# TensorE's order in the seven-product tiles of a decoder layer, and where GpSimd builds the block sums

## The chip, the cores and the metric

The kernel runs on one core of one Trainium2 chip. The metric is device time in microseconds (us) of one execution. TensorE does matmuls and transposes, VectorE and ScalarE move and combine what it leaves in its eight accumulation banks, GpSimd works on on-chip memory alone and issues some DMAs, and SyncE issues the other DMAs.

## The reference

One decoder layer for 8 sequences of 128 tokens, width 512, with a layer norm behind each of its three parts:

```python
x = _layernorm(x + _L0_attn_ref(x, L0_attn_Wq, L0_attn_Wk, L0_attn_Wv, L0_attn_Wo), axis=-1)
x = _layernorm(x + _L0_xattn_ref(x, ctx_4096, mask_BxSxS2_bk0, ...), axis=-1)
x = _layernorm(x + _L0_ffn_ref(x, L0_ffn_W_base, L0_ffn_b_base, ...), axis=-1)
```

The middle one is most of the time: cross attention with 32 heads of width 128.

```python
h_q = (x @ w_q.T).reshape(b, lq, H, DH)
h_k = (key_value_states @ w_k.T).reshape(b, lk, H, DH)
h_v = (key_value_states @ w_v.T).reshape(b, lk, H, DH)
score = jnp.einsum('bqhd,bkhd->bhqk', h_q, h_k)
score = score + position_bias[None]
score = jax.nn.softmax(jnp.where(m, score, -jnp.inf), axis=-1)
attn = jnp.einsum('bhqk,bkhd->bqhd', jnp.where(m, score, 0.0), h_v).reshape(b, lq, H * DH)
out = attn @ w_out.T
```

## The kernel before

Every projection is made of three matmul passes over split operands: a value is a high part and a low part (`hi`, `lo`), and the products hi·hi, lo·hi and hi·lo are summed in a bank. ScalarE writes the high part of a weight block, VectorE the low part.

The cross attention goes over 16 groups of two heads (`g` 0 to 15). A group has four tiles (`s` 0 to 3), one for a head and a half of the sequences. Tile number `n` is 4g+s. In tile n TensorE takes the scores of n, the transposes of the probabilities of n−1, the product of those with v (`pv`), two new v projections (`project_v`), and two output products (`output`) of earlier heads; between them lie the projections of q and k for later tiles.

In groups 0 and 1 ("plain") a tile projects q and k with twelve matmuls each (`project_q`, `project_k`). From group 2 on a group's q and k come from a scheme with seven block products in place of eight: `product_1` to `product_7`, each once for q (`w` = 0) and once for k (`w` = 1), with six matmuls of 128x512. Five of the right factors for each group are not the inputs but sums of input blocks, named S1k, S2k, S3k, S4k, S2q, S3q, S4q (and S1q, which stays on chip). GpSimd makes these sums once while groups 0 and 1 run, SyncE writes them to DRAM (`keep`, semaphores `s_kept`), and in every group GpSimd issues seven loads of 1 MB each into two ring slots (`load_sums`). A slot is reloaded when the product that read it is done: slot 0 holds S2q, S1k, S4k, S3k in turn, slot 1 holds S2k, S4q, S3q. The ring slots lie over four quarters of the buffer `stage`, `area(0)` to `area(3)`, in which GpSimd also builds the sums; `mem.u` is a further block of that size, used later by ScalarE for the copies of product 1 (`copy_p1`).

What sets the order is code written out by hand for each engine; each engine takes its instructions in that order and waits on semaphores. Two chains matter here. First, `bias_mask(g, s)` on GpSimd adds mask and bias for tile n into `bm`; VectorE's `masked_scores` of tile n waits for it (`s_bm`). GpSimd makes these adds between the block sums. Second, ScalarE in a plain tile takes `exps(n)` (which waits for VectorE's maxima), `copy_q`, `copy_k`, then `copy_prT(n-1)`; TensorE's `pv(n-1)` in the same tile waits for that last copy. VectorE turns the products into q and k (`sum_c11` and its like), and `normalise(n)` writes the probabilities.

A wait that both parts of the text speak of, in `product_6`:

```python
pe.wait_ge(s_op, done(OPS, g, "T2"))
pe.wait_ge(s_ring[SLOT_OF[name]], loaded(g, name))
pe.wait_ge(s_sum[w], done(SUMS, g, "C11"))
```

The weights' own sums T1 to T4 are GpSimd's (`three_turns`, `last_turn`), and T1 waits until the block A11 was split by VectorE.

Of the kernel before, what the change touches and what calls it, by code (L numbers as in the profile page):

```python
# [14 lines left out]
ALU = mybir.AluOpType  # L15
# [748 lines left out]
def layer(nc, a, sem, banks, mem, prev_a, out_d):  # L764
# [6 lines left out]
    with ExitStack() as ctx:  # L771
# [56 lines left out]
        BLOCKS = ("S1k", "S2k", "S4k", "S3k", "S3q", "S2q", "S4q")  # L828
# [13 lines left out]
        def loaded(g, name):  # L842

            order = SLOT_ORDER[SLOT_OF[name]]
            return 16 * len(order) * g + 16 * (order.index(name) + 1 - len(order) * SEVEN)
# [83 lines left out]
        def _(sp):  # L929
# [54 lines left out]

            sp.wait_ge(s_wv, 1)
# [10 lines left out]
            keep("S1k", stage[:, 0:2 * HALF * T], stage[:, 2 * HALF * T:4 * HALF * T])  # L996
            keep("S2k", stage[:, 0:2 * HALF * T], stage[:, 6 * HALF * T:8 * HALF * T])
# [4 lines left out]
            u_all = mem.u[:].rearrange("p i n -> p (i n)")  # L1002
            keep("S4k", stage[:, 2 * HALF * T:4 * HALF * T], u_all)
            keep("S3k", stage[:, 0:2 * HALF * T], stage[:, 4 * HALF * T:6 * HALF * T])
            keep("S3q", stage[:, 0:2 * HALF * T], stage[:, 6 * HALF * T:8 * HALF * T])
            sp.wait_ge(s_bm, TILES * 2)
            load_bias(2)
            keep("S2q", stage[:, 0:2 * HALF * T], u_all)
            keep("S4q", stage[:, 6 * HALF * T:8 * HALF * T], stage[:, 2 * HALF * T:4 * HALF * T])
# [28 lines left out]
        def _(pool):  # L1038
# [20 lines left out]
            def block_lo(name, out, raw, hi):  # L1059
                for c in range(2):  # L1060
                    nc.gpsimd.tensor_tensor(out[:, c], raw[:, c], f32(hi[:, c]), ALU.subtract).then_inc(s_ready, 1)  # L1061
                    pool.wait_ge(s_ready, 2 * BLOCKS.index(name) + c + 1)

# [17 lines left out]
            def k_first():  # L1081
                pool.wait_ge(prev_a.s_wout, B)
                pool.wait_ge(prev_a.s_xnlo, B)
                combine(U_, area(3), f32(quarter(cT[0], 0, 0)), ALU.add)
                combine(U_, U_, f32(quarter(cT[1], 0, 0)), ALU.add)
                hi_of(area(0, F32R), U_)
                block_lo("S1k", area(1, F32R), U_, area(0, F32R))

            def k_fourth():
# [1315 lines left out]
```

## Time and profile before

| | |
|---|---|
| median of 3 runs | 1098.26 us (1098.13 to 1098.43) |
| the profiled execution | 1096.46 us, of which the span from first to last instruction is 1094.5 us |
| mean granted TensorE clock | 0.988 |
| busy TensorE, VectorE | 1033.9 us (94%), 747.5 us (68%) |
| busy ScalarE, GpSimd | 500.6 us (46%), 488.0 us (45%) |

Busy time says who is nearest to being the bound. What a change is worth is read from the idle stretches of that engine and from what ended them. In this span the first self attention ends near 205 us, groups 0 and 1 run until about 318 us, groups 2 to 15 until about 1030 us, and the feed-forward part is the rest.

### The profile page before, as it was taken

The numbers are of one execution on the slowest core, as the hardware profiler recorded it, in microseconds if no ns is written. First come the engines' busy times: TensorE is split into PE (matmuls) and PEld (weight loads), VectorE is DVE, ScalarE is ACT, GpSimd is POOL, SyncE is SP. The second block draws the span as 40 slices with busy tenths as digits, with TensorE's granted clock in tenths as the row PEclk, the third lists the DMA queues.
The fourth block names the chain that finished last, engine by engine and source line by source line (L and its number), as shares of the span: only waits on it lengthen the run. The fifth ranks groups of instructions, "written<-read, shape, count | busy, mean of one in ns | idle before, by whom it ended". The sixth has DMA issues, their size and how long they took to land.

```text
span 1094.5 us, 20557 instructions
## 1 busy us (share of the span) xinstructions
PE 1033.9 (94%) x6354; PEld 895.0 (82%) x6354; DVE 747.5 (68%) x2269; ACT 500.6 (46%) x1377; POOL 488.0 (45%) x576
## 2 busy tenths in 40 slices
PE   7899988999689999999999999999999999999995
PEld 6677767888578888888888888888888888888884
DVE  6799988664557575757576666767575757576883
ACT  4889886454324343534343434444343435342421
POOL 7676665799954232423333242423242324232142
PEclk9999999999889999999999999999999999999998
DMA  4301002233375546372727374646455463737001
GB/s 150 126 21 50 2 1 69 78 117 120 124 259 185 193 157 235 115 249 101 258 98 286 99 255 142 242 142 227 164 186 192 157 236 113 249 101 243 19 20 58
DMA packets 44588, 159.77 MB, mean 146 GB/s; under 512 B 4736, under 2 KB 21504, under 8 KB 31616
## 3 DMA queue, kind: packets, MB, share of 16 engines
q0 software_dynamic: 14528, 105.91, 27.3%
q1 hardware_dynamic: 30016, 53.32, 14.5%
q8 instruction: 22, 0.36, 0.1%
q14 instruction: 22, 0.18, 0.0%
HBM read 149.78 MB, written 9.44 MB: 145 GB/s over the span
## 4 chain that ended last, share of the span: by engine, by line
PE 61%; POOL 13%; DVE 9%; DMA 8%; issue 7%; ACT 1%; POOLq 0%; DVEq 0%; SPq 0%; ACTq 0%
PE bank L1940 22%; PE bank L760 13%; PE bank L2094 11%; DMA ring<-block_sums 7%; PE bank L2081 4%; PE bank L2064 4%; PE bank L2112 3%; POOL stage L1053 3%; DVE sm L481 2%; PE bank L2071 2%; POOL u L1053 2%; POOL stage L1061 1%; POOL bm L1045 1%; POOL stage L1057 1%; POOL pool_gate L1070 1%
## 5 line engine op out<-in xcount | busy, mean ns | idle before, releaser
L1045 POOL TENSOR_TENSOR bm<-mask,bias 128x512 f32<-128x512 f32 x64 | 84.0, 1314 | 219.6 <-DVE nmx L1589 217.4
L1334 ACT ACTIVATE pr<-sm,nmx 128x128 f32<-128x128 f32 x256 | 99.8, 391 | 172.2 <-DVE nmx L1589 172.2
L1638 DVE TENSOR_TENSOR acc<-acc,bank 128x512 f32<-128x512 f32 x128 | 86.2, 684 | 78.0 <-PE bank L2094 78.0
L1070 POOL TENSOR_TENSOR pool_gate<-eps 128x1 f32<-128x1 f32 x96 | 44.1, 459 | 186.3 <-PE bank L1940 186.3
L1940 PE MATMUL bank<-ring,wqk_hi 128*128 128x512 f32 x392 | 112.1, 408 | 12.7 <-DMA ring<-block_sums 7.6
L1327 ACT COPY v<-bank 128x256 f32<-128x256 f32 x124 | 45.9, 370 | 127.7 <-PE bank L760 80.8
L2094 PE MATMUL bank<-wo_hi,at_hi 128*128 128x512 f32 x256 | 100.5, 393 | 0.3 <-DVE acc L1638 0.3
L2094 PE MATMUL bank<-wo_hi,at_lo 128*128 128x512 f32 x256 | 100.1, 391 | 0.1
L2094 PE MATMUL bank<-wo_lo,at_hi 128*128 128x512 f32 x256 | 100.0, 391 | 0.0
L1607 DVE TENSOR_TENSOR wqk_lo<-qk_raw,wqk_hi 128x512 fp32r<-128x512 f32 x98 | 88.4, 903 | 10.5 <-ACT wqk_hi L1364 10.5
L760 PE MATMUL bank<-wv_hi,cT_hi 128*128 128x256 f32 x512 | 88.9, 296 | 0.2 <-DVE wv_lo L1895 0.2
L1940 PEld LDWEIGHTS bank<-ring,wqk_hi 128*128 128x128 f32 x392 | 67.3, 191 | 25.2 <-issue 9.1
L760 PE MATMUL bank<-wv_hi,cT_lo 128*128 128x256 f32 x512 | 82.5, 284 | 0.0
L760 PE MATMUL bank<-wv_lo,cT_hi 128*128 128x256 f32 x512 | 82.3, 283 | 0.0
L1601 DVE TENSOR_TENSOR at_lo<-bank,at_hi 128x512 fp32r<-128x512 f32 x64 | 43.9, 686 | 55.3 <-ACT at_hi L1348 55.3
L1342 ACT COPY prT<-bank 128x512 f32<-128x512 f32 x64 | 37.3, 583 | 92.2 <-PE bank L2071 92.2
L760 PEld LDWEIGHTS bank<-wv_hi,cT_hi 128*128 128x128 f32 x512 | 72.7, 190 | 4.6 <-issue 0.4
L760 PEld LDWEIGHTS bank<-wv_hi,cT_lo 128*128 128x128 f32 x512 | 70.8, 192 | 0.0
L2064 PEld LDWEIGHTS bank<-kT,qT 128*128 128x128 f32 x512 | 66.7, 191 | 4.8
L760 PEld LDWEIGHTS bank<-wv_lo,cT_hi 128*128 128x128 f32 x512 | 70.5, 191 | 0.0
L2081 PE MATMUL bank<-prT,v 128*128 128x128 f32 x512 | 67.8, 275 | 1.3 <-ACT prT L1342 1.3
L2064 PE MATMUL bank<-kT,qT 128*128 128x128 f32 x512 | 67.3, 274 | 0.0
(289 smaller groups left out, 2620.8 us busy)
## 6 DMA issues: line engine op xcount, KB each, us to landing
ring<-block_sums POOLq DMA_DIRECT2D x98, 1024.0 KB, 5.2
qk_raw<-in_wqk SPq DMA_DIRECT2D x56, 256.0 KB, 5.6
o_raw<-in_wo SPq DMA_DIRECT2D x16, 512.0 KB, 3.3
v_raw<-in_wv SPq DMA_DIRECT2D x15, 512.0 KB, 8.7
block_sums<-stage SPq DMA_DIRECT2D x12, 512.0 KB, 3.2
acc<-in_x POOLq DMA_DIRECT2D x1, 2048.0 KB, 8.2
qk_raw<-in_wqk SPq DMA_DIRECT2D x4, 512.0 KB, 5.8
bias<-in_bias SPq DMA_DIRECT2D x16, 128.0 KB, 2.0
```

The source lines that it names most:

```text
L760: ins = nc.tensor.matmul(out, lhs, rhs, start=start and i == 0, stop=i == len(pairs) - 1)
L1045: nc.gpsimd.tensor_tensor(bm[:, s % 2], mask[:, HALF * (s // HG):HALF * (s // HG + 1), :], bias[:, i:i + 1, :].broadcast_to([P, HALF, T]), ...
L1053: made.link(nc.gpsimd.tensor_tensor(out[:, c], in0[:, c], in1[:, c], op))
L1070: nc.gpsimd.tensor_tensor(pool_gate[:, BLOCKS.index(name):BLOCKS.index(name) + 1], eps[:, 0:1], eps[:, 0:1], ALU.add)
L1327: nc.scalar.copy(v[:, b, :], PX[b % 2][:, 0:HG * DH2]).then_inc(s_vc, 1)
L1334: e = nc.scalar.activation(pr[:, s % 2, k], sm[:, s % 2, k], ACT.Exp, bias=nmx[:, s % 2, k:k + 1], accum_out=sums[:, s % 2, k:k + 1])
L1607: nc.vector.tensor_tensor(part_of(slot, 1), block_of(qk_raw, raw), f32(part_of(slot, 0)), ALU.subtract).then_inc(s_op, 1)
L1638: nc.vector.tensor_tensor(acc[:, b], acc[:, b], PX[b % 2][:], ALU.add).then_inc(s_acc, 1)
L1940: ins = nc.tensor.matmul((PQ, PK)[w][:], lhs, rhs, start=i == 0, stop=i == len(pairs) - 1)
L2064: ins = nc.tensor.matmul(S[s % 2][:, tok], qT[:, s % 2, tok], kT[:, s % 2, tok], start=True, stop=True)
L2081: ins = nc.tensor.matmul(PO[:, k * T:(k + 1) * T], v[:, half * HALF + k, i * DH2:(i + 1) * DH2], prT[:, k], start=True, stop=True)
L2094: ins = nc.tensor.matmul(PX[b % 2][:], at[p][:, half, i, tok], wo[q][:, i, :], start=k == 0 and (p, q) == PARTS[0], stop=k == HG - 1 and ( ...
```

## The change

It has two parts.

The order in the tiles of the seven-product scheme is now: scores, transposes of tile n−1, v, two products, `pv`, v, two products, outputs. Before, two products stood ahead of the transposes and the other two around the second v. In the last tile of a group product 6 for q comes ahead of `pv`, with the two products 2; in the first tile the two outputs alternate with the products 3. ScalarE copies the transposed probabilities ahead of the exponentials in these tiles, and VectorE's sums are put in an order to fit.

The block sums of the context are now made from the unsplit context. SyncE reads its first half again (two DMAs of 512 KB into `area(0)` and `area(1)`), ahead of the weights of group 1. GpSimd's order is new: `k_sums` has 8 instructions and `q_third` 6, and `bias_mask(1, 0)` stands behind the four splits of k and `q_third`. The last sum, S2q, is left in ring slot 0, from where product 6 of group 2 reads it.

```diff
+            sp.wait_ge(prev_a.s_wout, B)
+            for i in range(2):
+                sp.dma_start(area(i), mem.context_half(a["cT"], 0)[:, 2 * i:2 * i + 2]).then_inc(s_c_in, 16)
             sp.wait_ge(s_wv, 1)
             load_v(1)
...
-            def k_differences():
+            def k_sums():
                 pool.wait_ge(s_clo[0], 2)
                 pool.wait_ge(s_clo[1], 2)
-                combine(area(2), area(2), f32(quarter(cT[0], 0, 0)), ALU.subtract)
-                combine(area(2), area(2), f32(quarter(cT[1], 0, 0)), ALU.subtract)
-                combine(area(3), area(3), area(2), ALU.add)
+                pool.wait_ge(s_c_in, 48)
+                combine(area(0), area(2), area(0), ALU.subtract)
+                combine(area(2), area(2), area(3), ALU.add)
+                combine(area(3), area(3), area(0), ALU.add)
+                combine(area(1), area(1), area(3), ALU.subtract)
...
-            k_differences()
+            k_sums()
             bias_mask(0, 3, True)
-            k_first()
-            k_fourth()
-            k_second()
-            bias_mask(1, 0, False)
+            k_first_split()
+            k_second_split()
             k_fourth_split()
             k_third_split()
+            q_third()
+            bias_mask(1, 0, False)
+            q_second()
             bias_mask(1, 1, False)
-            q_third()
-            q_second()
-            bias_mask(1, 2, False)
             q_third_split()
             q_fourth()
-            bias_mask(1, 3, False)
             q_first()
-            q_second_split()
+            bias_mask(1, 2, False)
             q_fourth_split()
             q_first_split()
-            for name in BLOCKS[-2:]:
-                wait_kept(pool, name)
+            three_turns(SEVEN)
+            q_second_split()
             pool.wait_ge(s_s1q, 1)
-            load_sums(SEVEN, "S2q")
             load_sums(SEVEN, "S2k")
-            three_turns(SEVEN)
+            bias_mask(1, 3, False)
...
                 if isinstance(g, int) and g == SEVEN and w == 0:
-                    wait_kept(act, "S2q")
+                    wait_kept(act, "S3k")
...
+                scores(n, s, False, None if plain else g)
+                transposes(n - 1, sp)
+                new_v(g, n, b, c, weights)
+                if s == 0:
+                    product_5(g, 1)
+                    product_5(g, 0)
+                if s == 1:
+                    product_7(g, 0)
+                if s == 2:
+                    pair(product_4, g)
+                if s == 3:
+                    pair(product_2, g + 1)
+                    if not plain:
+                        product_6(g + 1, 0)
+                pv(n - 1, sp, head, v_ready, False)
+                new_v(g, n, b + 1, c + 1, weights)
+                if s == 0:
+                    product_3(g, 0)
+                    out(0)
+                    product_3(g, 1)
+                    out(1)
+                    return
```

TensorE at the start of a group from 3 on (tile s = 0). L2064 is the scores, L1940 with `ring_49` product 5 for k, which reads S1k, L2071 the transposes, L760 the v projection. Before:

```order
L2064 MATMUL bank<-kT,qT 128x128 [waits b_negmax]
L2064 MATMUL bank<-kT,qT 128x128 x3
L1964 REGISTER_ALU
L1968 ISA [waits b_operand]
L1969 REGISTER_ALU [waits b_sums_in_even]
L1940 MATMUL bank<-ring_49,wqk_hi 128x512 [waits b_k_product_summed]
L1940 MATMUL bank<-ring_49,wqk_hi 128x512 x3
L1940 MATMUL bank<-ring_49,wqk_lo 128x512 x2
```

The same place now, where L2068 is the scores, L2075 the transposes and L1941 the product:

```order
L2068 MATMUL bank<-kT,qT 128x128 [waits b_negmax]
L2068 MATMUL bank<-kT,qT 128x128 x3
L2075 MATMUL bank<-ident,pr 128x128 [waits b_probs]
L2075 MATMUL bank<-ident,pr 128x128 x3
L2185 REGISTER_ALU
L2186 ISA [waits b_wv]
L2187 REGISTER_ALU [waits b_acc]
L760 MATMUL bank<-wv_hi,cT_hi 128x256 [waits b_v_copied]
L760 MATMUL bank<-wv_hi,cT_hi 128x256 x3
L760 MATMUL bank<-wv_lo,cT_hi 128x256 x4
L760 MATMUL bank<-wv_hi,cT_lo 128x256 x4
```

The wait for the load of S1k (`b_sums_in_even`) moved behind the transposes and one v projection.

TensorE in the last tile of a group (s = 3), product 6 for q and `pv`. Before, with L2081 for `pv`:

```order
L2081 MATMUL bank<-prT,v 128x128 [waits b_at_lo,b_v_copied]
L2081 MATMUL bank<-prT,v 128x128 x3
L1958 REGISTER_ALU
L1959 ISA [waits b_operand]
L1940 MATMUL bank<-ring_49,wqk_hi 128x512 [waits b_q_product_summed,b_sums_in_even]
```

Now, with L2085 for `pv` and the products 2 for k just ahead:

```order
L1941 MATMUL bank<-cT_hi,wqk_lo 128x512 x2
L1959 REGISTER_ALU
L1963 ISA [waits b_operand]
L1941 MATMUL bank<-ring_49,wqk_hi 128x512 [waits b_q_product_summed,b_sums_in_even]
L1941 MATMUL bank<-ring_49,wqk_hi 128x512 x3
L1941 MATMUL bank<-ring_49,wqk_lo 128x512 x2
L2080 REGISTER_ALU [waits b_prT]
L2085 MATMUL bank<-prT,v 128x128 [waits b_at_lo,b_v_copied]
```

Product 6 for q moved ahead of `pv`, right behind products 2, whose sum it waits for (`b_q_product_summed`).

GpSimd while groups 0 and 1 run, from the wait for the context on. L1057 is `combine`, L1061 and L1065 the two steps of a split, L1049 `bias_mask`. Now:

```order
L1057 TENSOR_TENSOR stage<-stage 128x512 [waits b_ctx_in,b_ctx_lo_odd,b_ctx_lo_even]
L1057 TENSOR_TENSOR stage<-stage 128x512 [waits b_sums_made] x7
L1049 TENSOR_TENSOR bm<-mask,bias 128x512 [waits b_negmax,b_sums_made]
...
L1061 CAST u<-stage 128x512 [waits b_sums_kept_even,b_sums_ready]
...
L1057 TENSOR_TENSOR stage<-xnT_hi 128x512 [waits b_sums_ready]
L1057 TENSOR_TENSOR stage<-xnT_hi 128x512 [waits b_sums_made]
L1057 TENSOR_TENSOR stage<-stage,xnT_lo 128x512 [waits b_sums_made] x4
L1049 TENSOR_TENSOR bm<-mask,bias 128x512 [waits b_negmax,b_bias_in,b_sums_made]
```

The first instruction now waits for the DMA of the context (`b_ctx_in`), and the second `bm` shown, that of tile 4, stands behind 16 instructions of splits and 6 of `q_third`.

## Rows read from the trace of the kernel before

**Rows 1.** Waits from 284 to 318 us: us in total, times, longest

```profile
ACT u L1370 <- DMA block_sums<-u: 13.3, 1, 13.3
...
PE bank L1940 <- ACT u L1370: 8.1, 1, 8.1
...
PE bank L1940 <- DVE wqk_lo L1607: 4.5, 1, 4.5
```

**Rows 2.** Windows on TensorE: length, busy (instructions), granted clock, DMA share, GB/s

```profile
297.40:301.80 4.40, 4.31 (x12) 0.62 0.92 331
...
309.20:315.90 6.70, 6.63 (x25) 0.61 0.51 152
```

**Rows 3.** Timeline of TensorE, scores of four tiles and the next: start, us

```profile
629.26 1.05 PE L2064 MATMUL bank<-kT,qT 128*128 128x128 f32 x8
...
643.53 1.05 PE L2064 MATMUL bank<-kT,qT 128*128 128x128 f32 x8
...
667.51 1.05 PE L2064 MATMUL bank<-kT,qT 128*128 128x128 f32 x8
...
680.92 1.05 PE L2064 MATMUL bank<-kT,qT 128*128 128x128 f32 x8
```

**Rows 4.** Line 1071: first the issue at 624.4 us (S1k), then S4k

```profile
DMA to landing us min/median/max: 6.4/6.4/6.4
...
L1071 POOL DMA_DIRECT2D ring<-block_sums x1: 577/577/577, 633.1 to 633.1; - x1
...
DMA to landing us min/median/max: 5.1/5.1/5.1
```

**Rows 5.** Timeline of a tile s = 1, and VectorE's first instruction behind `normalise`

```profile
591.87 1.05 PE L2064 MATMUL bank<-kT,qT 128*128 128x128 f32 x8
...
594.62 1.08 PE L1940 MATMUL bank<-ring,wqk_hi 128*128 128x512 f32 x4
...
596.01 1.05 PE L2081 MATMUL bank<-prT,v 128*128 128x128 f32 x8
...
596.85 0.69 DVE L1607 TENSOR_TENSOR wqk_lo<-qk_raw,wqk_hi 128x512 fp32r<-128x512 f32 x1
...
598.34 1.08 PE L1940 MATMUL bank<-ring,wqk_hi 128*128 128x512 f32 x4
```

**Rows 6.** SyncE's second DMA from 210 us on; a load of 1 MB behind one of 512 KB

```profile
210.65 0.37 SPq L935 DMA_DIRECT2D v_raw<-in_wv  x1
...
stage<-in_cT SPq DMA_DIRECT2D x1, 1024.0 KB, 7.5
```

**Rows 7.** Timeline of GpSimd: sums, a mask, one split

```profile
209.81 2.64 POOL L1053 TENSOR_TENSOR stage<-stage,cT_hi 128x512 f32<-128x512 f32 x2
...
218.31 1.30 POOL L1045 TENSOR_TENSOR bm<-mask,bias 128x512 f32<-128x512 f32 x1
...
244.31 1.29 POOL L1057 CAST stage<-u 128x512 fp32r<-128x512 f32 x2
...
248.40 1.29 POOL L1057 CAST stage<-stage 128x512 fp32r<-128x512 f32 x2
```

**Rows 8.** DMAs issued at 232.5 to 233 us, writes of S1k

```profile
block_sums<-stage SPq DMA_DIRECT2D x2, 512.0 KB, 3.1
```

**Rows 9.** Timeline of tile 4 on VectorE, ScalarE and TensorE

```profile
246.04 0.28 DVE L1584 CUSTOM_DVE_ANT_0 sm<-bank,bm 128x128 f32<-128x128 f32 x1 [0.21 <-issue]
...
247.21 0.41 ACT L1334 ACTIVATE pr<-sm,nmx 128x128 f32<-128x128 f32 x1 [4.44 <-DVE nmx L1589]
...
248.84 0.59 ACT L1317 COPY qT<-bank 128x512 f32<-128x512 f32 x1
...
253.26 1.06 PE L2081 MATMUL bank<-prT,v 128*128 128x128 f32 x8
```

**Rows 10.** Timeline of tile 6: the scores, and VectorE's splits of A11 and A22

```profile
271.71 1.05 PE L2064 MATMUL bank<-kT,qT 128*128 128x128 f32 x8
...
279.98 3.18 DVE L1607 TENSOR_TENSOR wqk_lo<-qk_raw,wqk_hi 128x512 fp32r<-128x512 f32 x2 [0.20 <-ACT wqk_hi L1364]
```

More of the change, by code:

```diff
@@ L827, in layer @@
         SLOT_ORDER = [[n for n in SLOT_OF if SLOT_OF[n] == k] for k in range(2)]
-        BLOCKS = ("S1k", "S2k", "S4k", "S3k", "S3q", "S2q", "S4q")
+        BLOCKS = ("S1k", "S2k", "S4k", "S3k", "S3q", "S4q", "S2q")
         UNITS = ("p1", "p2", "p6", "p5", "p3", "p7", "p4")
@@ L995, in _ @@
             load_v(2)
-            keep("S1k", stage[:, 0:2 * HALF * T], stage[:, 2 * HALF * T:4 * HALF * T])
-            keep("S2k", stage[:, 0:2 * HALF * T], stage[:, 6 * HALF * T:8 * HALF * T])
+            u_all = mem.u[:].rearrange("p i n -> p (i n)")
+            flat = [stage[:, k * 2 * HALF * T:(k + 1) * 2 * HALF * T] for k in range(4)]
+            keep("S1k", u_all, flat[2])
+            keep("S2k", u_all, flat[3])
+            keep("S4k", flat[2], flat[1])
+            keep("S3k", u_all, flat[0])
             for i in range(HG):
@@ L1001, in _ @@
                 load_block(SEVEN, name)
[L1002 to L1005, printed above, removed]
+            keep("S3q", flat[0], flat[3])
+            keep("S4q", flat[0], flat[1])
+            keep("S2q", *[f32(mem.ring[0][:, p].rearrange("p c n -> p (c n)")) for p in range(2)])
             sp.wait_ge(s_bm, TILES * 2)
             load_bias(2)
-            keep("S2q", stage[:, 0:2 * HALF * T], u_all)
-            keep("S4q", stage[:, 6 * HALF * T:8 * HALF * T], stage[:, 2 * HALF * T:4 * HALF * T])
             sp.wait_ge(s_wo, 2)
@@ L1269, in first_half @@
                 bias_mask(g, 3, False)
+            wait_kept(pool, "S2q")
             second_half(SEVEN)
@@ new lines, in seven_step, with short_step @@
+                if s == 2 and not last:
+                    pair(product_1, g + 1)
+                if s == 3 and plain:
+                    product_6(g + 1, 0)
+                if s == 3:
+                    product_6(g + 1, 1)
+                out(0)
+                out(1)
+            def short_step(g, s):
+                n, sp = TILES * g + s, (s - 1) % TILES
+                scores(n, s, False, g)
+                if s == 1:
+                    pair(product_7, g)
+                transposes(n - 1, sp)
+                for j in range(2):
+                    pe.wait_ge(s_acc, 2 * n - 5 + j)
+                    output((HALF + 2 * s + j) % B, s // HG ^ 1 if s < 2 else 0, (1, 0) if s < 2 else (0, 1))
+                    if j == 0:
+                        pv(n - 1, sp, FRESH_B[sp], B * g + HALF * (sp // HG + 1), False)
@@ L2202, in step @@
                         continue
+                    if last and s in (1, 3):
+                        short_step(g, s)
+                        continue
+                    if not plain or (s == 3 and not plain_next):
+                        seven_step(g, s, last, plain)
+                        continue
                     sp = (s - 1) % TILES
                     had_out = not (first and s < 3)
-                    head = heads_of(first or (s == 0 and plain))[sp]
-                    order = (0, 1) if s >= 2 or plain else (1, 0)
@@ L2213, in out @@
+                    for j in range(2):
+                        pe.wait_ge(s_vc, 2 * n + HALF + j + 1)
                         if j == 0 and s == 2:
                             pe.wait_ge(s_wo, g + 1)
[L2215 to L2223 removed]
@@ L2238, in step @@
-                    for j in range(2):
-                        pe.wait_ge(s_vc, 2 * n + HALF + j + (-1 if moved else 1))
-                        out(j)
-                    if plain and not plain_next and s == 2:
-                        product_1(g + 1, 0)
-                        product_1(g + 1, 1)
+                        output((HALF + 2 * s + j) % B, 0 if s >= 2 else 1, (0, 1), n if j == 0 and s in (0, 2) else None)
+                    if not plain_next and s == 2:
+                        pair(product_1, g + 1)
```

175 lines of the change are left out of this document (84 added, 91 removed).

## The prediction

> **What bounds the kernel now.** I read the page's busy shares first (TensorE 94%), then TensorE's waits, then the timeline around the longest. TensorE is the bound almost everywhere, so only its idle stretches and slow stretches can be won. They lie in two places.
>
> The first is where group 2 takes over from the plain groups. ScalarE's copy of product 1 waited 13.3 us for the write of S2q to DRAM, and TensorE waited 8.1 us for that copy, then 4.5 us for a VectorE split that hung on GpSimd's late weight sums [rows 1]. Behind each stall the granted clock was low: 4.40 us at 0.62 and 6.70 us at 0.61, a mix of the 1.2 and 2.4 GHz levels [rows 2]. At 0.62 the work done in 4.40 us is worth 2.7 us, so 1.7 us were lost, and in the second window 2.6 us. The place costs 8.1 + 4.5 + 1.7 + 2.6 = 16.9 us.
>
> The second recurs in each group. The tile s = 0 lasts 643.53 − 629.26 = 14.27 us, and the tile s = 3, which has the same instructions in number and shape (scores, transposes, two v, four products, `pv`, two outputs), 680.92 − 667.51 = 13.41 us [rows 3]. The 0.86 us between them is the wait of product 5 for S1k, whose load took 6.4 us [rows 4]. In a group of 51.66 us that is all the idle time.
>
> **The change, steady groups.** The matmuls are the same in number. In the order scores, transposes, v, product, which the tile s = 1 already has, the product starts at +2.75 us from the scores and takes 596.01 − 594.62 = 1.39 us; from `pv` to the product behind the next v it is 2.33 us [rows 5].
>
> - Product 5 for k now starts at +2.75 in place of about +0.8, and product 6 for q, which frees the slot, ends earlier: before at 2 × 1.39 + 1.39 behind transposes, v and `pv`, now without `pv` ahead (0.8 us). The load of S1k gets 1.9 + 0.8 us more against a lateness of 0.86. The wait goes: −0.86 us a group.
> - Product 6 for q now starts at 2.75 + 2 × 1.39 = +5.53 in the last tile, and waits for VectorE's sum of product 2. VectorE now takes `normalise` first and comes free at 596.85 − 591.87 = +4.98; the sum takes as long as the 0.69 us beside it and ends at +5.67 [rows 5]. That is 0.14 late, and the start behind a wait costs some 0.1 to 0.2 us more, as the weight load can't run ahead: +0.3 us. Below nothing it can't go; if ScalarE's exponentials slip it is 0.6.
> - Product 3 for k starts at 5.53 + 2.33 + 1.39 + 1.37 (an output, six matmuls of the same width) = +10.6. Its block S4k is loaded when product 5 for k is done, at +4.14, through GpSimd's queue, so issued near +5.0. It took 5.1 us when issued at 633.13 [rows 4], so it lands at +10.1, and the weight load would be due at +10.4. I take 0.06 us for it; it is the thinnest cover of the change.
> - Outputs, copies by ScalarE ahead of the exponentials (the transposes end before VectorE has the maxima), and the reordered adds lie under TensorE's work: nothing.
>
> Net −0.86 + 0.3 + 0.06 = −0.5 us a group. The tile s = 0 counts 13 times (groups 3 to 15) and so does product 6: −6.5 us, between −2.6 (0.2 a group) and −8 (0.6).
>
> **The change, start of group 2.** GpSimd has three `combine` less (6 instructions), TensorE needs S2q later and from the ring slot where it was made, and ScalarE no longer waits for its write. But the sums start later.
>
> - The context copies are issued behind `load_o(0)`, where the second DMA now stands, at 210.65 [rows 6]. A load of 1 MB of this context behind one of 512 KB took 7.5 us [rows 6], so both halves are there at 218.2. GpSimd was ready at 209.8 [rows 7]. It waits 8.4 us, more than the 8.4 us that the six instructions saved are worth (209.81 to 218.31 for six, 1.4 each [rows 7]).
> - From there: `k_sums`, 8 × 1.4 = 11.2, to 229.4. Mask of tile 3, 1.3, to 230.7. Split of S1k 4.1 (244.31 to 248.40 for one [rows 7]), to 234.8. The next split writes into `mem.u`, which S1k's write reads: 0.4 for the second issue and 3.1 for the landing [rows 8], to 238.3. Three splits, 12.3 and 0.3 for a wait on S2k's write, to 250.9. `q_third`, 6 × 1.4 = 8.4, to 259.3. Mask of tile 4, 1.3, to 260.6.
> - VectorE wanted that mask at 246.04 [rows 9]; it is 14.6 us late. Behind it in a plain tile: maxima 1.17 (to 247.21), exponentials 1.63 (to 248.84), `copy_q`, `copy_k` at a pitch of about 0.5, `copy_prT` 0.6 as the copies beside it, together 4.4. So `pv` starts at 265.0 in place of 253.26 [rows 9]: +11.7 us. Low clock behind the stall: 1.7 and 2.6 stand in the rows for the old ones; I take 2.5, at most 3.4. Shift 14.2.
> - GpSimd's next pieces have room: masks of tiles 5 and 6 come before their shifted tiles. Tile 6 starts at 285.9. VectorE's split of A11 ended 9.9 us behind its scores (279.98 + 1.6 − 271.71 [rows 10]): 295.8. Three weight sums at 1.4, S2q's split 4.1: 304.1. Mask of tile 7 to 305.9, when its scores (302.5) are 3.4 old. Maxima 1.2, exponentials 1.6, the copy of T2 0.6, `normalise` and the split of T2 about 1.6: 310.9. Product 6 would be due at 302.5 + 5.53 + 2.33 = 310.4: a wait of 0.5, in place of the old 4.5. S2k, issued near 304.6, lands near 310 to 312, in time.
> - Tile 8 starts near 316.6 (302.5 + 13.4 + 0.5, and 0.2 for a start behind a wait). S1k is issued near 312.9 and by 6.4 us [rows 4] lands at 319.3, just when product 5 is due. GpSimd's queue and SyncE's weight loads are fuller at this place, so I allow 0.8 us of wait, between 0 and 1.7.
>
> So the old 16.9 us and the 0.86 go, and 11.7 + 2.5 + 0.5 + 0.8 come. That is 17.8 − 15.5 = 2.3 us gained. Bounds: GpSimd and VectorE slow each other (VectorE's split takes 1.6 us in the one place and 0.69 in the other [rows 10, 5]); with GpSimd's mean piece at 1.6 the mask comes at 264, +3.4 and some clock, a loss near 2; with every piece at 1.3 it comes at 259, a gain near 4.
>
> **A rule beside it.** The load of 1 MB behind 512 KB took 7.5 us [rows 6]. The Trainium skill (DMA: Bandwidth & Descriptors, "Specifications" and "Anatomy of one DMA") puts the fixed part at about 2 us and the ceiling of one core's DMA at 435 GB/s; by an estimate from it the context is there near 216, 2.2 us sooner, and the time would be 1087.3 us. No row here shows that rate for this load.
>
> **The sum.** −2.3 − 6.5 = −8.8 us. The profiled execution (1096.46 us, its span 1094.5) becomes 1087.7, and its distance of 1.8 us to the median of the three runs is kept: 1098.26 − 8.8 = 1089.5 us.
>
> **The rivals.**
>
> 1. *The mask is not late enough to matter.* If the context were there when GpSimd is ready, the chain would end 8.4 us sooner and leave a stall of 3.3 us with no lasting loss of clock: −8.4 − 2.5 = −11 beyond the forecast, 1078.6 us. For it: SyncE's queue was empty when the copies are issued. Against it: the copies can't be issued before the last transposes of the first part, at 210.2. Chance 0.14.
> 2. *Slower: S4k decides.* The thinnest cover is product 3 for k. The load is issued near +5.0 and must land by +10.4, so the point is 5.4 us; it took 5.1, but S1k's took 6.4 with other loads in flight [rows 4]. At 6.4 each of the 14 first tiles waits 1.0 and some 0.15 for the start: +16 us, 1105 us. It turns the sign from 6.1 us on. For it: S3q's and S4k's loads stand nearer together now. Against it: S4k's neighbour has nearly landed at that point. Chance 0.14.
> 3. *Nothing measurable.* The chain on GpSimd ends at 264 to 266 and the groups give only 0.2: 2 + 1 − 2.6, about 1098.5 us. For it: GpSimd's pieces doubled beside VectorE's. Against: VectorE idles while it waits for this very mask. Chance 0.12.
>
> The forecast has 0.60.
>
> **How the numbers follow.** The forecast's own range is 1084 to 1094.5 (−4 and −8 from the low bounds with some of the clock; +2 and −2.6 with some clock on the other side). The range 1077.5 to 1099 takes in rivals 1 and 3 and leaves out rival 2 and some tails, under 2 in 10. A change within 0.2% (2.2 us) is about what can't be told from none. Faster: 0.60 + 0.14 + a little of rival 3 and less 0.02 of tails, 0.74. Same: 0.10. Slower: 0.16.
>
> **What the changed profile would show.** GpSimd's first `combine` waits until about 218 for a DMA. The mask of tile 4 ends near 260.6. TensorE waits once near 253 to 265 for `prT`, and the stalls of 8.1 and 4.5 us are gone. In each group the tile s = 0 lasts 13.4 to 13.6 us, and product 6 in the last tile waits 0.1 to 0.4 us for VectorE. It is wrong if the context lands much off 218, if a plain tile has more slack than 4.4 us behind its mask, or if a ring load is waited for in every group.

## The result and the profile after

The changed kernel takes 1117.73 us (1116.52 to 1119.63), against 1098.20 us of the kernel before on the same chip: ratio 1.0182, interval 1.0164 to 1.0200, slower. The forecast was 1089.5 us, and the range ended at 1099. The profiled span grew from 1094.5 to 1115.6 us, 21.1 us. TensorE runs the same 6354 matmuls, and its busy time grew by 6.6 us (1033.9 before):

```profile
span 1115.6 us, 20550 instructions
...
PE 1040.5 (93%) x6354; PEld 895.5 (80%) x6354; DVE 730.6 (65%) x2269; ACT 498.0 (45%) x1377; POOL 487.9 (44%) x569
```

So the work didn't grow. Two thirds of the loss is idle time, and the rest is matmuls that ran slower (the mean granted clock went from 0.988 to 0.985, and it is low behind long stalls, as shown below). The starts of the scores of each tile, read from TensorE's timeline of both kernels, say where (these are differences of rows like those of [rows 3]):

| stretch | before, us | after, us | difference |
|---|---|---|---|
| tile 0 to tile 9 | 136.58 | 143.14 | +6.6 |
| tiles s = 0 of groups 3 to 15, mean of 13 | 14.26 | 14.51 | +0.25 |
| tiles s = 1, mean of 13 | 10.60 | 10.67 | +0.07 |
| tiles s = 2, mean of 13 | 13.38 | 13.70 | +0.32 |
| tiles s = 3, mean of 13 | 13.41 | 13.73 | +0.32 |

(The tiles s = 1 to 3 are those of groups 2 to 14, so the four rows are one stretch without a gap.) The groups lose 0.96 us each, 12.5 us in 13. The rest is 0.9 us ahead of tile 0, where nothing was changed, and 1.2 us in the last group. Tile 0 starts anywhere from 195.7 to 197.6 us in the twelve traces of this document, so the 0.9 us is scatter. The 1.2 us stand in the last group of every run with the new order, and most of them are two products in its tile s = 1 that wait 1.5 us together, where one waited 0.6 before. The forecast had −6.5 for the groups and −2.3 for the start of group 2.

**The start of group 2.** Waits from 205 to 330 us in the kernel after (us in total, times, longest), to be held against [rows 1]:

```profile
DVE spare L51 <- POOL bm L1049: 17.1, 1, 17.1
...
PE bank L2085 <- ACT prT L1339: 15.6, 3, 13.9
...
POOL stage L1057 <- DMA stage<-in_cT: 8.7, 1, 8.7
...
POOL bm L1049 <- issue: 7.3, 1, 7.3
...
POOL u L1061 <- DMA block_sums<-stage: 4.1, 1, 4.1
...
PE bank L1941 <- DMA ring<-block_sums: 3.8, 1, 3.8
```

The old stalls of 8.1 and 4.5 us are gone. In their place stand `pv` behind the mask of tile 4 (13.9) and product 5 behind the load of S1k (3.8). GpSimd's timeline shows the chain behind the first (start, us, what it waited for):

```profile
209.04 1.74 POOL L1049 TENSOR_TENSOR bm<-mask,bias 128x512 f32<-128x512 f32 x1
219.43 13.87 POOL L1057 TENSOR_TENSOR stage<-stage 128x512 f32<-128x512 f32 x8 [8.65 <-DMA stage<-in_cT]
...
243.69 1.29 POOL L1061 CAST u<-stage 128x512 fp32r<-128x512 f32 x2 [4.08 <-DMA block_sums<-stage]
...
264.00 1.26 POOL L1049 TENSOR_TENSOR bm<-mask,bias 128x512 f32<-128x512 f32 x1
...
308.74 0.61 POOL L1075 DMA_DIRECT2D ring<-block_sums  x1 [0.30 <-POOL ring L1065]
309.38 1.30 POOL L1049 TENSOR_TENSOR bm<-mask,bias 128x512 f32<-128x512 f32 x1
317.93 1.30 POOL L1049 TENSOR_TENSOR bm<-mask,bias 128x512 f32<-128x512 f32 x1 [7.26 <-issue]
```

Read from the top: GpSimd is ready at 210.8 and waits for the context until 219.4; `k_sums` takes 13.87 us; the write of S1k is waited for; the mask of tile 4 ends at 265.3. TensorE's timeline of that tile:

```profile
247.34 1.05 PE L2068 MATMUL bank<-kT,qT 128*128 128x128 f32 x8
...
269.73 2.08 PE L2085 MATMUL bank<-prT,v 128*128 128x128 f32 x8 [13.91 <-ACT prT L1339]
...
276.68 0.49 PE L2068 MATMUL bank<-kT,qT 128*128 128x128 f32 x3
```

The tile lasts 29.34 us, 15.95 more than before. The `pv` takes 2.08 us in place of 1.05: the granted clock is low behind the stall (0.61 from 269 to 275 us).

**A steady group.** The tile s = 0 that starts at 537.21, the longest, lasts 15.41 us. On TensorE, product 5 for k, product 3 for q and the first output run without a gap, and then:

```profile
537.21 1.05 PE L2068 MATMUL bank<-kT,qT 128*128 128x128 f32 x8
...
539.96 1.08 PE L1941 MATMUL bank<-ring,wqk_hi 128*128 128x512 f32 x4
...
545.08 1.08 PE L1941 MATMUL bank<-ring,wqk_hi 128*128 128x512 f32 x4
...
549.73 1.20 PE L1941 MATMUL bank<-ring,wqk_hi 128*128 128x512 f32 x4 [1.73 <-DMA ring<-block_sums]
```

The product at +2.75 us (539.96) waits for nothing, as the prediction said: the wait for S1k is gone. The one that waits is product 3 for k, for S4k. That load was issued at 541.73 (the line of the load, from issue to landing):

```profile
L1075 POOL DMA_DIRECT2D ring<-block_sums x1: 580/580/580, 541.7 to 541.7; - x1
...
DMA to landing us min/median/max: 8.0/8.0/8.0
```

This is group 6 (tile 24). The load took 8.0 us where [rows 4] has 5.1. In groups 3 to 14 of this trace it took 6.0 to 8.0 us, the middle one 7.2. SyncE's timeline shows what is new beside it: the weight block d goes out at 540.41, 1.3 us ahead of S4k, because VectorE now splits T3 before its other work. Before, it went out 0.2 to 1.0 us behind the load of S4k.

```profile
540.41 4.38 SPq L964 DMA_DIRECT2D qk_raw<-in_wqk  x2
```

The 0.32 us of s = 3 are the wait of product 6 for q, and those of s = 2 a wait that I hadn't looked for. VectorE and TensorE around the start of a tile s = 2 (scores at 563.22):

```profile
564.11 0.60 PE L2075 MATMUL bank<-ident,pr 128*128 128x128 f32 x4
564.85 0.73 PE L760 MATMUL bank<-wv_hi,cT_hi 128*128 128x256 f32 x4
```

```profile
562.11 0.67 DVE L1610 TENSOR_TENSOR u<-bank,u 128x512 f32<-128x512 f32 x1
562.71 1.42 DVE L1573 TENSOR_TENSOR wv_lo<-v_raw,wv_hi 128x1024 fp32r<-128x1024 f32 x1
564.05 1.27 DVE L1636 TENSOR_TENSOR acc<-acc,bank 128x512 f32<-128x512 f32 x2
```

The v projection could start at 564.47 (0.36 behind the transposes, as in the other tiles) and starts at 564.85. Its bank is free only when the first of the two adds is done, near 564.7. In the old order two products 4 stood ahead of it and covered this.

### The profile page after: what moved, and what is told of

Its sections match the earlier page's. It is cut to its first block, busy times and chain, and to the rows that moved or that the text cites. A ratio compares the mean times of both kernels' runs of the same rounds, so it can differ in the third digit from the quotient of the medians.

```text
span 1115.6 us, 20550 instructions
## 1 busy us (share of the span) xinstructions
PE 1040.5 (93%) x6354; PEld 895.5 (80%) x6354; DVE 730.6 (65%) x2269; ACT 498.0 (45%) x1377; POOL 487.9 (44%) x569
## 4 chain that ended last, share of the span: by engine, by line
PE 39%; issue 12%; DMA 8%; DVE 7%; POOL 3%; ACT 2%; DVEq 0%; POOLq 0%; ACTq 0%
PE bank L1941 17%; DMA ring<-block_sums 8%; PE bank L760 7%; PE bank L2098 7%; PE bank L2116 3%; PE bank L2085 2%; POOL bm L1049 2%; PE bank L2068 2%; ACT pr L1331 2%; DVE wqk_lo L1605 1%; DVE acc L1636 1%; PE bank L2075 1%; DVE u L1610 1%; DVE wv_lo L1573 1%; DVE sm L1582 1%
## 5 line engine op out<-in xcount | busy, mean ns | idle before, releaser
L1049 POOL TENSOR_TENSOR bm<-mask,bias 128x512 f32<-128x512 f32 x64 | 99.5, 1555 | 205.9 <-DVE nmx L1587 196.5
L1074 POOL TENSOR_TENSOR pool_gate<-eps 128x1 f32<-128x1 f32 x96 | 38.4, 400 | 214.4 <-PE bank L1941 214.3
L1941 PE MATMUL bank<-ring,wqk_hi 128*128 128x512 f32 x392 | 110.4, 403 | 20.4 <-DMA ring<-block_sums 15.5
L1605 DVE TENSOR_TENSOR wqk_lo<-qk_raw,wqk_hi 128x512 fp32r<-128x512 f32 x98 | 79.0, 807 | 33.4 <-ACT wqk_hi L1361 33.4
L1941 PEld LDWEIGHTS bank<-ring,wqk_hi 128*128 128x128 f32 x392 | 67.5, 190 | 41.0 <-DMA ring<-block_sums 16.8
L760 PE MATMUL bank<-wv_hi,cT_hi 128*128 128x256 f32 x512 | 92.5, 303 | 1.8 <-DVE acc L1636 0.3
L2085 PEld LDWEIGHTS bank<-prT,v 128*128 128x128 f32 x512 | 67.3, 193 | 22.0 <-ACT prT L1339 17.1
L2085 PE MATMUL bank<-prT,v 128*128 128x128 f32 x512 | 68.7, 278 | 16.2 <-ACT prT L1339 16.2
L760 PE MATMUL bank<-wv_lo,cT_hi 128*128 128x256 f32 x512 | 82.2, 283 | 0.0
L760 PE MATMUL bank<-wv_hi,cT_lo 128*128 128x256 f32 x512 | 82.2, 283 | 0.0
L760 PEld LDWEIGHTS bank<-wv_hi,cT_hi 128*128 128x128 f32 x512 | 69.7, 191 | 5.0 <-issue 4.7
L2068 PEld LDWEIGHTS bank<-kT,qT 128*128 128x128 f32 x512 | 66.7, 191 | 4.8
L760 PEld LDWEIGHTS bank<-wv_hi,cT_lo 128*128 128x128 f32 x512 | 70.6, 191 | 0.0
L760 PEld LDWEIGHTS bank<-wv_lo,cT_hi 128*128 128x128 f32 x512 | 70.2, 190 | 0.0
L1345 ACT CAST at_hi<-bank 128x512 fp32r<-128x512 f32 x64 | 37.7, 589 | 69.5 <-PE bank L2085 69.5
```

The costliest lines, as they stand in the source:

```text
L760: ins = nc.tensor.matmul(out, lhs, rhs, start=start and i == 0, stop=i == len(pairs) - 1)
L1049: nc.gpsimd.tensor_tensor(bm[:, s % 2], mask[:, HALF * (s // HG):HALF * (s // HG + 1), :], bias[:, i:i + 1, :].broadcast_to([P, HALF, T]), ...
L1074: nc.gpsimd.tensor_tensor(pool_gate[:, BLOCKS.index(name):BLOCKS.index(name) + 1], eps[:, 0:1], eps[:, 0:1], ALU.add)
L1345: nc.scalar.copy(at[0][:, s // HG, i], PO[:]).then_inc(s_ah, 1)
L1605: nc.vector.tensor_tensor(part_of(slot, 1), block_of(qk_raw, raw), f32(part_of(slot, 0)), ALU.subtract).then_inc(s_op, 1)
L1941: ins = nc.tensor.matmul((PQ, PK)[w][:], lhs, rhs, start=i == 0, stop=i == len(pairs) - 1)
```

## Experiments

Runs of one batch share a chip and their runs of the kernel before; medians of before went from 1096.2 to 1098.2 us between batches, so I compare ratios to before. The changed kernel has 1.0182.

**1 and 2: the two halves apart.** The first has the new tile order of TensorE (here its core), ScalarE and VectorE on the old sums. The second has the new `BLOCKS`, `keep` and GpSimd order (here its core) and the read of S2q from the ring, on the old tile order.

```diff
+                    if not plain or (s == 3 and not plain_next):
+                        seven_step(g, s, last, plain)
+                        continue
```

```diff
-            k_differences()
+            k_sums()
...
-            load_sums(SEVEN, "S2q")
...
-                pe.wait_ge(s_ring[SLOT_OF[name]], loaded(g, name))
+                if isinstance(g, int) and g == SEVEN and w == 0:
+                    pe.wait_ge(s_ready, 2 * len(BLOCKS))
```

> The kernel before with the new tile order alone (TensorE, ScalarE, VectorE); GpSimd and SyncE build the block sums as before. Theory A (the groups lose about 1.0 us each because of the tile order: product 3 for k waits for the load of S4k, the tiles s = 2 and s = 3 wait 0.3 us each for VectorE): 1098.2 + 12.5, and at the start of group 2 the old stalls with some change of either sign, so 1108 to 1113 us, and the tiles s = 0, 2, 3 last about 14.5, 13.7 and 13.7 us as in the changed kernel. Theory B (the groups lose because of where the last sums lie and what the ring loads meet, that is because of both parts together): the tiles of the groups from 3 on last 13.4 to 13.8 us with no ring wait, and the time is 1092 to 1099 us.

> The kernel before with the new building of the block sums alone (SyncE reads the context again, GpSimd's new order, S2q left in the ring); the tile order is the old one. Theory A (this part costs what the first groups lost, the groups from 3 on stay at 14.26, 10.60, 13.38 and 13.41 us a tile): a wait of about 14 us for the mask of tile 4, the old stalls of 8.1 and 4.5 us mostly gone, 1102 to 1107 us. Theory B (the old order in tiles 7 and 8 wants product 6 and S1k sooner than the new one, so the late S2q costs more here): over 1109 us.

The order alone took 1111.69 us, 1.0117 (1.0081 to 1.0152); the sums alone 1103.68 us, 1.0060 (1.0041 to 1.0078). The two add up to 1.0177, so within these intervals no interaction shows. In the order alone the tiles of groups 3 to 15 last 14.75, 10.60, 13.75 and 13.74 us, and tile 0 to 9 takes 0.9 us less than before. In the sums alone they last 14.14, 10.60, 13.38 and 13.41 us, as before, and tile 0 to 9 takes 7.9 us more. In the order alone the load of S4k took 6.9 to 8.2 us in groups 3 to 14, but 5.1 us in group 6. Theory A held on both. The stall of the sums alone, with the old order around it:

```profile
267.31 2.07 PE L2081 MATMUL bank<-prT,v 128*128 128x128 f32 x8 [13.94 <-ACT prT L1339]
```

**3: the masks moved up.** All four masks of group 1 go ahead in GpSimd's order, the first into the wait for S1k's write.

```diff
             k_first_split()
+            bias_mask(1, 0, False)
             k_second_split()
             k_fourth_split()
             k_third_split()
+            bias_mask(1, 1, False)
             q_third()
-            bias_mask(1, 0, False)
             q_second()
-            bias_mask(1, 1, False)
+            bias_mask(1, 2, False)
...
-            bias_mask(1, 2, False)
+            bias_mask(1, 3, False)
             q_fourth_split()
```

> The changed kernel with the four masks of group 1 moved up among GpSimd's block sums, the first one into the 4.1 us in which GpSimd waits for the write of S1k. Theory A (what bounds the first groups is GpSimd's whole chain from the context's landing at 219 to the split of S2q at 308; the mask's wait only hides it): tile 4 lasts 13.4 us, but product 6 of group 2 then waits 6 to 10 us for S2q, and the kernel gains 4 to 9 us of 1117.7: 1109 to 1114 us. Theory B (the late mask of tile 4 is the cost itself, as the prediction priced it, 11.7 + 2.5 and more): gain of 14 to 16 us, 1102 to 1104 us, with no long wait at product 6.

It took 1114.99 us, 1.0155 (1.0127 to 1.0183), 2.7 thousandths better than the changed kernel, though the intervals overlap. Tile 4 is back at 13.38 us, but tile 7 went from 15.65 to 33.22:

```profile
307.84 2.05 PE L1941 MATMUL bank<-ring,wqk_hi 128*128 128x512 f32 x4 [10.59 <-issue]
...
315.73 2.04 PE L1941 MATMUL bank<-ring,wqk_hi 128*128 128x512 f32 x4 [4.99 <-issue]
```

Product 6 for q waits for the split of S2q, which ends near 307.8 on GpSimd, and product 6 for k for the load of S2k, issued at 308.04 and landed 7.6 us later. So the mask was only where the lateness showed first; what bounds this place is GpSimd's whole chain. Theory A's mechanism held. Its gain (4 to 9) was too high, and the time lies 1 us above its range. One reason is the second wait, which I had left out. Another stands in the trace: tile 0 to 9 takes 2.7 us less than in the changed kernel, but tile 12 lasts 17.01 us in place of 14.23. There product 3 for k waits 1.8 us for S4k, and the mean granted clock from 384 to 392 us is 0.84.

**4: block d behind S4k.**

```diff
-                sp.wait_ge(s_op, done(OPS, g, "T3"))
-                load_block(g + 1, "d")
                 sp.wait_ge(s_op, done(OPS, g, "T4"))
+                load_block(g + 1, "d")
                 load_block(g + 1, "b")
```

> The changed kernel, but SyncE loads the weight block d only when T4 is split, 2.7 us behind the issue of S4k in place of 1.3 us ahead of it. Theory A (the load of S4k took 8.0 us in place of 5.1 because this 256 KB stands ahead of it): S4k lands in 5 to 6.5 us, product 3 for k waits 0 to 0.3 us, the tiles s = 0 last 13.4 to 13.8 us, and the time is 1105 to 1110 us against 1117.7. Theory B (it is the sum of the traffic around it, S4q, v and the blocks, wherever block d stands): S4k still takes over 7 us, the tiles s = 0 last about 14.5 us, 1116 to 1119 us.

1112.50 us, 1.0146 (1.0122 to 1.0171). The load of S4k in group 6 (issued at 539.04):

```profile
L1074 POOL DMA_DIRECT2D ring<-block_sums x1: 580/580/580, 539.0 to 539.0; - x1
...
DMA to landing us min/median/max: 5.5/5.5/5.5
```

5.5 in place of 8.0 in this group. Over groups 3 to 14 the load took 5.2 to 7.6 us, the middle one 6.5 (in the changed kernel 7.2), so one group says little. The tiles s = 0 fell from 14.51 to 13.93 us on average; six of 13 are at 13.4, the others still wait. Block d was half of it. Neither theory held: 13.93 us and 1112.5 us lie above the ranges of A and below those of B.

**5: VectorE's two places.**

```diff
                     sum_c22(g, 1)
-                    sum_z(g, 1)
+                    accumulate(n, 0, (HALF + 2 * s) % B)
                     lo(wv, v_raw, s_wv_h, s_wv, g + 2)
+                    sum_z(g, 1)
+                    accumulate(n, 1, (HALF + 2 * s + 1) % B)
+                    return
...
-                    normalise(n, s, link)
                     sum_c11(g + 1, 0)
+                    normalise(n, s, link)
                     sum_c11(g + 1, 1)
```

> The changed kernel with two changes of VectorE's order: in the tile s = 1 the first add of the outputs and the split of wv come ahead of the sum z for k, and in the tile s = 3 the sum C11 for q comes ahead of normalise. Theory A (the v projection of s = 2 waits 0.37 us for its bank behind these, and product 6 for q 0.27 us behind normalise): the tiles s = 2 and s = 3 go from 13.70 and 13.73 to 13.4 us, 13 times each, and the kernel from 1117.7 to 1109 to 1111 us if nothing else moves. Theory B (a wait of the same length appears behind it, for the split of wv in s = 2 or for the sum u1 in s = 0): the tile s = 2 stays above 13.6, or s = 0 grows by as much, 1115 us or more.

1106.66 us, 1.0084 (1.0052 to 1.0116). The tiles s = 2 and s = 3 last 13.33 and 13.37 us, 0.36 each less than in the changed kernel, and s = 0 stays at 14.43. Both waits were as named. The time is 2 us below the expected range; the two tiles explain 9.5 of the 10.8 us gained.

**6: v behind S4k too.** The edit of 4, and v behind the blocks.

```diff
-                sp.wait_ge(s_wv, g + 1)
-                load_v(g + 1)
...
                 load_block(g + 1, "d")
                 load_block(g + 1, "b")
+                sp.wait_ge(s_wv, g + 1)
+                load_v(g + 1)
```

> The changed kernel with SyncE's loads of d, b and then v all behind the split of T4, so that neither d nor the 512 KB of v lie ahead of S4k. Theory A (S4k's landing is set by what was issued ahead of it): S4q lands in 6 to 7 us in place of 8.9, S4k in 5.1 to 5.5 in place of 8.0, all tiles s = 0 last 13.4 us, 13 times 1.1 us less than the changed kernel, 1102 to 1105 us against 1117.7. Theory B (v behind S4k shares its bandwidth as well, and only the sum counts): no better than with block d alone behind S4k, s = 0 at 13.9 us on average, 1110 to 1114 us.

1101.46 us, 1.0038 (1.0024 to 1.0053). All 13 tiles s = 0 last 13.42 or 13.43 us. The landing of all loads of the sums from 340 to 1020 us, the changed kernel's first, then this one's:

```profile
DMA to landing us min/median/max: 5.0/5.2/9.1
```

```profile
DMA to landing us min/median/max: 5.0/5.2/7.6
```

The S4k of group 6, issued at 535.71, took 5.1 us, and in groups 3 to 14 it took 5.1 to 5.4. So the landing of S4k was set by d and v, which were issued ahead of it, and 13.42 us is what the prediction had promised for this tile. Two things stay open. With v away, S4q, which goes out 6.9 us ahead of S4k from GpSimd too, lands in 5.5 to 7.6 us in place of 8.3 to 9.1; whether v holds up S4k itself or by way of S4q isn't shown. And v now goes out 3.9 us behind S4k, so the two overlap for some 1.3 us only: the run shows what it is worth to issue v late, and not whether the order of issue or the traffic in the same time counts.

**7: the order alone, mended.** Experiment 1 with the edits of 5 and 6.

> The new tile order with the old building of the block sums, and the three things that cost it time mended: d, b and v behind the split of T4, and VectorE's two places. Theory A (these three waits are all that the order costs): the tiles last 13.4, 10.6, 13.4 and 13.4 us, that is 50.8 in place of 51.65 us a group before, 13 times 0.85 = 11 us, with the start of group 2 as in the order alone (0.9 us less than before): 1085 to 1088 us against 1097.5 to 1098. Theory B (the mended waits come back somewhere, a load of v or of the blocks that is now late, or a slower clock): 1092 us or more.

1085.72 us (1084.55 to 1086.95), ratio 0.9895 (0.9875 to 0.9915): faster than both kernels. The tiles last 13.43, 10.84, 13.33 and 13.37 us, 50.97 a group in place of 51.65, which is 8.9 us in 13 groups, and tile 0 to 9 takes 2.5 us less. Of TensorE's waits from 340 to 1020 us this is all that is left:

```profile
PE bank L1946 <- issue: 1.5, 2, 1.2
PE bank L2077 <- DVE pr L1595: 0.9, 1, 0.9
PE bank L1946 <- DMA ring<-block_sums: 0.5, 1, 0.5
```

The tile s = 1 is 0.24 us longer than before. It is the price of moving v: it now goes out 1.3 us ahead of S3q, the next load, in place of 6.6 us ahead of S4k. In tile 9, the longest with 12.09 us, product 7 for q waited for S3q, which was issued at 326.61 and took 7.9 us:

```profile
334.54 1.19 PE L1946 MATMUL bank<-ring,wqk_hi 128*128 128x512 f32 x4 [1.24 <-DMA ring<-block_sums]
```

In a steady group S3q is issued 9.65 us behind the start of the tile s = 0 and wanted 16.2 us behind it, so it has 6.5 us. In tile 57, with 11.43 us, it took 7.2; in tiles 21 and 25, with 10.60, it took 6.1 and 6.0. Experiment 6 has the same waits, among others in tiles 9, 17 and 21.

**8: the old order with v late.** Could the load's side alone have won the 0.86 us?

```diff
-                sp.wait_ge(s_wv, g + 1)
-                load_v(g + 1)
                 sp.wait_ge(s_op, done(OPS, g, "T3"))
                 load_block(g + 1, "d")
                 sp.wait_ge(s_op, done(OPS, g, "T4"))
                 load_block(g + 1, "b")
+                sp.wait_ge(s_wv, g + 1)
+                load_v(g + 1)
```

> The kernel before with nothing changed but SyncE's load of v, which stands behind the block b. The old wait for S1k in the tile s = 0 (0.86 us a group) is attacked from the load's side. Theory A (S1k took 6.4 us because blocks a, c and v were issued beside it, and v is the largest): S1k lands in 5.2 to 5.8 us, the tiles s = 0 last 13.4 to 13.7 us in place of 14.26, 13 times 0.6 to 0.85, and the kernel gains 8 to 11 us: 1087 to 1090 us. Theory B (it is the blocks a and c that are issued with it that count, v comes 1.4 us later): S1k still takes 6.2 to 6.4 us and nothing is gained, 1097 to 1099 us.

1095.73 us, 0.9989 (0.9975 to 1.0002): no difference. The tiles s = 0 stay at 14.28 us, and S1k takes 6.1 to 6.5 us in groups 3 to 14, where it took 6.0 to 6.4 before. Theory B: v went out 1.4 us behind S1k there and held it little. The same load matters for S4k since by then it is 6.6 us old and still not down (8.8 us in the changed kernel). So the gain of 7 needs the new order. (The time is 1 us below what theory B expected, with the kernel before at 1096.85 in this batch.)

**9: no reload of the context.** The sums are then made from whatever the two areas hold; only the time is read.

```diff
-            sp.wait_ge(prev_a.s_wout, B)
-            for i in range(2):
-                sp.dma_start(area(i), mem.context_half(a["cT"], 0)[:, 2 * i:2 * i + 2]).then_inc(s_c_in, 16)
...
-                pool.wait_ge(s_c_in, 48)
+                pool.wait_ge(prev_a.s_wout, B)
```

> The changed kernel without SyncE's second load of the context's first half and without the wait for it; the sums are made from what area(0) and area(1) hold, so the output is another and only the time is read. It asks what the lateness of the context costs. Theory A (GpSimd's chain starts 8 to 9 us sooner, at 211, and all of it comes sooner by that): the wait for the mask of tile 4 falls from 13.9 to some 5 us, tile 2 is back at 13.6 us, and the kernel is 9 to 12 us faster than 1117.7: 1106 to 1109 us. Theory B (the chain is held by other things, the write of S1k and VectorE's large splits beside it, and gives the 8 us back on its way): the wait in tile 4 stays over 9 us, the gain is under 6 us.

1108.58 us, 1.0117 (1.0100 to 1.0134). GpSimd starts at once, and TensorE's wait in tile 4 shrinks from 13.91 to 8.09 us:

```profile
209.87 12.05 POOL L1054 TENSOR_TENSOR stage<-stage 128x512 f32<-128x512 f32 x8
```

```profile
260.77 2.08 PE L2082 MATMUL bank<-prT,v 128*128 128x128 f32 x8 [8.09 <-ACT prT L1336]
```

The kernel gains 6.5 thousandths, 7 us, between the two theories (9 to 12, and under 6). `k_sums` starts 9.6 us sooner, and the mask of tile 4 comes 264.00 − 255.05 = 8.95 us sooner. The wait shrinks by 5.8 us only, since TensorE is at this place 3.1 us sooner as well. Tile 2 went from 15.18 to 13.39 us: in the changed kernel the load of v stood behind the context's in SyncE's order, was issued at 212.51 and took 8.0 us, and `pv` waited 1.1 us. The context's lateness is thus worth 7 us. Without it the ratio is that of the order alone (1.0117 both), so even then the new sums win nothing.

**10: everything mended.** The whole change with the edits of 3, 5 and 6.

> The whole change with everything mended that the runs showed: the masks moved up, SyncE's d, b and v behind the split of T4, VectorE's two places. Theory A (the gains add up: 2.7 of the masks, 13 times 1.1 in s = 0, 13 times 0.7 in s = 2 and 3): 1117.7 - 26 = about 1091.5 us, 1089 to 1094, that is faster than before but 4 to 8 us slower than the order alone mended (1085.7), the price of the new block sums. Theory B (with the order mended the late S2q and the loads of the first groups cost more): over 1095 us.

1090.69 us, 0.9949 (0.9935 to 0.9963). Inside theory A's range. The groups last as in 7 but for s = 1 (10.66), and tile 7 takes 32.85 us. The mended order with the old sums is 5.4 thousandths faster, near 6 us. So the new sums cost about what experiment 2 said (6.0 thousandths), though here with the masks moved up.

## Why the prediction was wrong

**The step that failed** is the one that gave product 3 for k 0.06 us: "It took 5.1 us when issued at 633.13 [rows 4], so it lands at +10.1". The issue was put at +5.0 and came at +4.52, and product 3 was due at +10.6, as forecast, so the cover was some 6 us and not 5.4. But the load took 7.2 us in the middle of groups 3 to 14 (8.0 in the group shown), and the tile s = 0 was 1.1 us too long on average (14.51 against 13.42), 14.2 us over the 13 groups. I took a duration from the old trace for a load whose neighbours the change had moved. Experiments 4 and 6 show it: the load takes 6.5 us in the middle once d is issued behind it, and 5.2 once v is too, and the tile is at 13.42. The change's part in it was VectorE's new order, which put the split of T3 first and so sent block d out ahead; v was under way at S4k's issue before too, but landed 0.6 to 1.8 us behind it, and now 1.6 to 2.4. The prediction counted the reordered adds as "nothing" and doesn't name this split. One row was also too few: in the old trace this load took 5.1 or 5.2 us in nine of groups 3 to 14, but 5.9 to 6.1 in three, where d went out 0.2 us behind it.

Rival 2 named this wait, with the price of a load of 6.4 us, 1.15 us a tile, and a total of 1105. It named a nearer S3q and loads in flight as grounds, and neither d nor v. That its price came out right (1.1) is luck: the load took 0.8 us more than its 6.4, and the cover was some 0.6 us more as well. Its chance of 0.14 was too low for the term that I called the thinnest cover. Its total is still 13 us too low, for what follows.

**The second miss** is the sentence that the copies and adds "lie under TensorE's work: nothing". In the tile s = 2 the first v projection moved ahead of two products, and its bank was still with VectorE: 0.36 us a group in experiment 5, 4.7 us in all. What should have been asked of v, as of every moved instruction: whose work frees its bank, and when does that end?

**Right:** in groups 3 to 15 the wait for S1k went, product 5 starts at +2.75, and product 6 waits for VectorE (+0.3 forecast, 0.32 measured, 0.36 given back in experiment 5).

**The start of group 2.** Forecast 2.3 us gained, measured 6.6 lost.

- The mask of tile 4 ended at 265.3 in place of 260.6. The context came at 219.4 (218.2 forecast, with all of this kernel 0.9 us later, as tile 0 is). The pieces of `k_sums` were the term that was most mis-sized: 1.73 us each in place of 1.4, 2.7 us for the eight. I had put this at the edge of the range ("with GpSimd's mean piece at 1.6"). The split of S1k took 5.0 us in place of 4.1, and the wait for its write 4.1 in place of 3.5. From the mask's end to `pv` it took 4.5 us, as forecast (4.4). Stall and low clock came to 15.95 us in place of 14.2.
- Tile 2 and 3 lost 1.5 us, since v's load stands behind the context's. The prediction followed what waits for the context and not what was queued behind it.
- Tile 7 took 15.65 us against 14.1 forecast: product 6 for q waited 1.2 us for VectorE's split of T2, and that for k another 0.6, for the load of S2k, which was issued at 308.74 and took 8.9 us.
- Tile 8 took 18.87 us against 14.2: product 5 waited 3.8 us for S1k and then ran at a low clock. S1k was issued at 321.8, not 312.9. GpSimd issues it behind the masks of tiles 8 and 9, the first of these waits for the bias of group 2, and SyncE loads that bias only behind the mask of tile 7, at 310.70; it took 7.1 us beside the load of S2k and the writes of S2q. That is the 7.3 us row above. The forecast had a wait of 0.8 there and named fuller queues, but not the instruction that stood ahead.

The first, third and fourth stand on one long chain, that of GpSimd, and experiment 3 shows that it is late to its end: with the masks out of it, TensorE waits 10.6 + 5.0 us there. The forecast followed this chain from the mask of tile 4 to that of tile 7, but priced only the wait that showed at each stop. Its own text has one slip that changes nothing: GpSimd's wait of 8.4 us is as long as the six instructions saved, and not longer.

The estimate beside the forecast, that the context is there near 216, was too early: its loads were issued at 211.57, and the first sum started at 219.43. The row of 7.5 us was the better guide.

## What to carry to other kernels

A transfer's duration belongs to the traffic around it: when a change moves it, or moves any issue near it on another queue, cost it anew, above all where its cover is under one microsecond, and read it in every group of the old trace and not in one. For each instruction that moves earlier, list what frees its operands and its bank, and not only what it was waiting for before. And where a chain on a helper engine is late, find its end before pricing its first stall: repairing the visible wait of 16 us gave some 3.

## What the runs showed of the hardware

How long the 1 MB load of S4k took hung on what was under way, in groups 3 to 14 (shortest, middle, longest):

| what else was issued | us |
|---|---|
| v (512 KB) 6.6 us and d (256 KB) 1.3 us ahead of it (changed kernel) | 6.0, 7.2, 8.0 |
| v 6.6 us ahead, d 2.7 us behind (experiment 4) | 5.2, 6.5, 7.6 |
| d 2.7 us and v 3.9 us behind (experiment 6) | 5.1, 5.2, 5.4 |

The spread within a row is as large as the step from one row to the next, so d's place alone doesn't fix it. At the 341 GB/s below, 256 KB are worth 0.8 us. In the group shown above (8.0 us) the rate fell late in the load, with S4k, S3q and the block b out:

```profile
541.73:546.73 5.00, 5.00 (x34) 4.47 (x33) 3.27 (x6) 1.23 (x3) 0.59 (x3) 1.00 0.87 276
546.73:548.73 2.00, 1.27 (x6) 0.72 (x4) 1.23 (x2) 0.00 (x0) 0.71 (x2) 1.00 0.48 118
```

The last columns are the granted clock, the DMA share and GB/s of all the core's transfers; before, in the 5.1 us of S4k's load from 581.51 on, they moved 341 GB/s. Why the DMA engines were half idle for 2 us with work outstanding stays open. The Trainium skill (DMA: Bandwidth & Descriptors, "Queues, rings and completion order") says that each DMA engine goes round the queues by packets, and that the count which reports a landing waits for every earlier write of that engine, across its queues. The runs agree with the direction (loads on SyncE's queue delay one on GpSimd's), and none tells the two mechanisms apart.

GpSimd's additions in `k_sums` took 1.28 to 2.22 us. The five that touch the stretch from 224.0 to 231.5 us, beside VectorE's work (7.27 of 7.50 us busy, with splits of 1024 elements a partition), had a median of 2.14:

```profile
L1057 POOL TENSOR_TENSOR stage<-stage x5: 1303/2138/2224, 222.2 to 230.3; 128x512 f32<-128x512 f32 x5
```

The Trainium skill (SBUF — State Buffer, "SBUF: two separate sides") has a port pair that VectorE and GpSimd hold in turn for a whole instruction, also where VectorE reads two inputs from that memory. The trace agrees: the three of 2.14 to 2.22 us, from 222.2 to 228.8, stand beside three such splits, and the next took 1.30. The old trace had two such pieces of 2.25 us from 219.6 us on, just where the forecast had put `k_sums`; they would have priced it better than the mean of the six before them.
